# Experts of a decoder layer: weight blocks stationary, rows moving, in the first matrices

## The chip, the cores and the metric
The kernel runs on one core of a Trainium2 chip. The metric is the device time of one execution in microseconds; three executions of the kernel before gave 1971.84, 1976.12 and 1981.54 us, median 1976.12.

## The reference
One decoder layer on x of 8 sequences, 512 tokens, 256 channels: causal self-attention with 16 heads, cross-attention with 16 heads, and then a block with its own small attention, a router and experts. The last of them is what the change touches. After the norm, each of the 4096 tokens goes to two of eight experts:

```
h  = silu(x @ eW1[e].T) * (x @ eW3[e].T)     # 256 -> 256 each
eo = h @ eW2[e].T
out += combine[t, e] * eo                    # for the token's two experts
```

All in float32; the kernel keeps that accuracy with float16 parts: a matrix and its operand are each split into a high and a low part, and a product is three matmuls (high by high, low weight by high operand, high weight by low operand).

## The kernel before
The kernel has three stages, each a block of five engine programs with orders of their own, tied by semaphores: `self_attention`, `cross_attention` with `moe_attention` behind it, and `moe_experts`. The change is in `moe_experts` (lines 2626 to 2920) alone.

Ahead of it, tokens have been written to DRAM sorted by expert, as rows of 256 high parts, 256 low parts and some marks. They are cut into tiles of 128 rows, each of one expert, and two tiles make a pair. There are 40 pairs (NP; 28 of the first six sequences, 12 of the last two), and all loops run over pairs, fully unrolled. Which expert a tile has is known on the chip only: `expert_of` (line 2698) has PE's sequencer load the number from a table in SBUF into a register, and the weights `w13` (first matrices, eW1 and eW3 side by side, 512 columns for each of two 128-row halves kc) and `w2` are addressed with that register. Such a register address is worked out by instructions of PE's sequencer, in the stream between the matmuls.

For a pair p:
- SP loads the two tiles (128 rows each) into `xr` (`first_keys` in the profile, whose memory it uses), up to four pairs ahead.
- PE, `turn_rows` (2692): 8 transposes of 128x128 into `pX`; ACT, `rows_out` (2758), copies them to `xt`.
- PE, `hidden` (2708): for each of the two tiles 6 matmuls, the transposed rows `xt` stationary and 512 columns of `w13` moving, into `pH`: tokens on partitions, 256 values of eW1 and 256 of eW3 along the row. Amid it stand the look-ups of the next pair's experts, and `turn_rows(p + 1)` between the two tiles.
- ACT, `tanh` (2764); DVE, `activate` (2789, 2792), two operations of 512 elements; ACT, `high` (2769); POOL, `low` (2849): the two float16 parts `H16` of the hidden values.
- PE, `turn_hidden` (2725): 8 transposes into `pT`; DVE, `hidden_out` (2798), copies them to `ht`.
- PE, `make` (2736): for each tile 6 matmuls with `ht` stationary and 256 columns of `w2` moving, into `pO`; ACT, `made_out` (2774), to `eo`; POOL, `send_back` (2855), two indirect DMAs a pair to `back` in DRAM.

PE's order is written out by hand: `hidden(p)`, `turn_hidden(p - 1)`, `make(p - 2)`. DVE also works out where results go (`places`, 2817 and 2824), builds a table, and in the last eight or so pairs adds six returned blocks a pair to the residual (`combine`, 2806). Behind the last pair, the rest of the results come back, are combined and stored. A wait is written with `after` (line 28). On PE the waits and the register work run on its sequencer.

Of the kernel before, what the change touches and what calls it, by code (L numbers as in the profile page):

```python
# [8 lines left out]
F16 = mybir.dt.float16  # L9
# [5 lines left out]
P = 128  # L15
T = 512
C = 256
CK = C // P
# [6 lines left out]
def after(eng, sem, n):  # L25

    if n > 0:
        eng.wait_ge(sem, n)

class Names:
# [5 lines left out]
    def sb(self, name, shape, dt):  # L37
        return self.mem.enter_context(self.nc.sbuf_tensor(f"{self.prefix}_{name}", shape, dt))
# [4 lines left out]
    def sem(self, name):  # L43
        return self.keep.enter_context(self.nc.semaphore(f"{self.prefix}_{name}"))
# [2581 lines left out]
def moe_experts(nc, keep, mem, k, x_res, out_dram, B, groups, shared):  # L2626
# [3 lines left out]
    sb, sem = names.sb, names.sem  # L2630

    def banks(name, n):
        return mem.enter_context(nc.psum_tensor(f"e_{name}", [P, n, T], F32))

    w13, w2, weight, back = shared["w13"], shared["w2"], shared["weight"], shared["back"]
# [4 lines left out]
    xt = sb("xt", [P, 2, 2, 2, CK, P], F16)  # L2640
    TH = sb("TH", [P, 2, 2, C], F32)
    H16 = [sb(f"H16_{n}", [P, 2, 2, C], F16) for n in ("hi", "lo")]
    ht = sb("ht", [P, 2, 2, 2, CK, P], F16)
    eo = sb("eo", [P, EB, 2, C], F32)
    odd = sb("odd", [P, IB, 2], F32)
    back_to = sb("back_to", [P, IB, 2], mybir.dt.uint32)
# [2 lines left out]

    pX = banks("pX", 1)  # L2650
    pH = [banks("pH0", 2), banks("pH1", 2)]
    pT = banks("pT", 1)
    pO = [banks("pO0", 1), banks("pO1", 1)]

    s_xt, s_xe, s_h, s_th, s_a, s_hh = sem("xt"), sem("xe"), sem("h"), sem("tanh"), sem("a"), sem("hh")
    s_hi, s_lo, s_ht, s_he, s_o, s_eo = sem("hi"), sem("lo"), sem("ht"), sem("he"), sem("o"), sem("eo")
    s_odd, s_bt = sem("odd"), sem("back_to")
    s_st = [sem(f"stored{n}") for n in range(EB)]
    s_ga, s_cmb, s_out = [sem(f"came_back{n}") for n in range(4)], sem("combined"), sem("out")
# [3 lines left out]
    NP = len(pairs)  # L2663
# [19 lines left out]
    def tensor_program(eng):  # L2683
        expert = {}

        def turn_rows(p):
            eng.wait_ge(s_ld[p % XB], 32 * (p // XB + 1))
            after(eng, s_xe, p)
            for h in range(2):
                for c in range(4):  # L2690
                    o = (h * 4 + c) * P
                    m = eng.transpose(pX[:, 0, :].bitcast(F16)[:, o:o + P], xr[:, p % XB, h, c * P:(c + 1) * P], k.id16[:, :])  # L2692
            m.then_inc(s_xt, 1)

        def expert_of(p, h):
            if p < NP:
                n, q = pairs[p]
                expert[p, h] = eng.value_load(tables.row(n, 0, 2 * q + h), min_val=0, max_val=ER - 1) + 1

        def hidden(p):  # L2700
            eng.wait_ge(s_xe, p + 1)
            after(eng, s_hh, p - 1)
            for h in range(2):
                e = expert[p, h]
                i = 0
                for kc in range(CK):
                    for x, ww in ((0, 0), (0, 1), (1, 0)):
                        m = eng.matmul(pH[p % 2][:, h, :], xt[:, p % 2, h, x, kc, :],  # L2708
                                       w13[ww][:, kc, bass.ds(e, 1), :].rearrange("p a f -> p (a f)"), start=(i == 0), stop=(i == 5))
                        i += 1  # L2710
                        if i == 3:
                            expert_of(p + 1, h)
                if h == 0 and p + 1 < NP:
                    turn_rows(p + 1)
            m.then_inc(s_h, 1)

        def turn_hidden(p):
            eng.wait_ge(s_hi, p + 1)
            eng.wait_ge(s_lo, p + 1)
            after(eng, s_he, p)  # L2720
            for h in range(2):
                for x in range(2):
                    for c in range(CK):
                        o = (h * 4 + x * 2 + c) * P
                        m = eng.transpose(pT[:, 0, :].bitcast(F16)[:, o:o + P], H16[x][:, p % 2, h, c * P:(c + 1) * P], k.id16[:, :])  # L2725
            m.then_inc(s_ht, 1)

        def make(p):
            eng.wait_ge(s_he, p + 1)
            after(eng, s_eo, p - 1)  # L2730
            for h in range(2):
                e = expert[p, h]
                i = 0
                for c in range(CK):
                    for x, ww in ((0, 0), (0, 1), (1, 0)):
                        m = eng.matmul(pO[p % 2][:, 0, h * C:(h + 1) * C], ht[:, p % 2, h, x, c, :],  # L2736
                                       w2[ww][:, bass.ds(e, 1), c, :].rearrange("p a f -> p (a f)"), start=(i == 0), stop=(i == 5))
                        i += 1
            m.then_inc(s_o, 1)

        for h in range(2):
            expert_of(0, h)
        turn_rows(0)
        for p in range(NP):
            hidden(p)
            if p >= 1:
                turn_hidden(p - 1)
            if p >= 2:
                make(p - 2)
        make(NP - 2)  # L2750
        turn_hidden(NP - 1)
        make(NP - 1)

    def scalar_program(eng):
        def rows_out(p):
            eng.wait_ge(s_xt, p + 1)
            after(eng, s_h, p - 1)
            eng.activation(xt[:, p % 2, :, :, :, :].rearrange("p h x k t -> p (h x k t)"), pX[:, 0, :].bitcast(F16),  # L2758
                           ACT.Copy).then_inc(s_xe, 1)

        def tanh(p):
            eng.wait_ge(s_h, p + 1)
            after(eng, s_lo, p - 1)
            eng.activation(TH[:, p % 2, :, :], pH[p % 2][:, :, 0:C], ACT.Tanh, scale=0.5 / WS).then_inc(s_th, 1)

        def high(p):
            eng.wait_ge(s_hh, p + 1)
            after(eng, s_ht, p - 1)
            eng.activation(H16[0][:, p % 2, :, :], TH[:, p % 2, :, :], ACT.Copy).then_inc(s_hi, 1)  # L2769

        def made_out(p):
            eng.wait_ge(s_o, p + 1)
            after(eng, s_st[p % EB], 32 * (p // EB))
            eng.activation(eo[:, p % EB, :, :].rearrange("p h c -> p (h c)"), pO[p % 2][:, 0, :], ACT.Copy).then_inc(s_eo, 1)

        rows_out(0)
        for p in range(NP + 2):
            if p + 1 < NP:
                rows_out(p + 1)
            if p < NP:  # L2780
                tanh(p)
                high(p)
            if p >= 2:
                made_out(p - 2)

    def vector_program(eng):
        def activate(p):
# [3 lines left out]
            eng.wait_ge(s_a, p + 1)  # L2791
            eng.scalar_tensor_tensor(out=TH[:, p % 2, :, :], in0=pH[p % 2][:, :, C:2 * C], scalar=0.5 / WS ** 2,  # L2792
                                     in1=TH[:, p % 2, :, :], op0=ALU.mult, op1=ALU.mult).then_inc(s_hh, 1)

        def hidden_out(p):
            eng.wait_ge(s_ht, p + 1)
            after(eng, s_o, p - 1)
            eng.tensor_copy(ht[:, p % 2, :, :, :, :].rearrange("p h x k t -> p (h x k t)"), pT[:, 0, :].bitcast(F16)).then_inc(s_he, 1)

        def combine(i):  # L2800
            b, t, n = returns[i]
# [28 lines left out]
        for p in range(NP + 2):  # L2830
            if p < NP:
                activate(p)
            if 1 <= p <= NP:
                hidden_out(p - 1)
            if p + 1 < NP:
                places(p + 1)
            for _ in range(TABLED):
                next(table, None)
            if p >= 2:
                for i in returns_at(p - 2):  # L2840
                    combine(i)
# [3 lines left out]
    def gpsimd_program(eng):  # L2845
        def low(p):
            eng.wait_ge(s_hi, p + 1)
            after(eng, s_ht, p - 1)
            eng.tensor_tensor(H16[1][:, p % 2, :, :], TH[:, p % 2, :, :], H16[0][:, p % 2, :, :], ALU.subtract).then_inc(s_lo, 1)  # L2849

        def send_back(p):
            eng.wait_ge(s_eo, p + 1)
            eng.wait_ge(s_bt, 2 * (p + 1))
            for h in range(2):
                eng.indirect_dma_start(out=back[:, :], out_offset=bass.IndirectOffsetOnAxis(ap=back_to[:, p % IB, h:h + 1], axis=0),  # L2855
                                       in_=eo[:, p % EB, h, :], in_offset=None).then_inc(s_st[p % EB], 16)

        def scatter(t):

            b = B - 1  # L2860
            for n in range(2):
                eng.indirect_dma_start(out=groups[1].sent[:, :],
                                       out_offset=bass.IndirectOffsetOnAxis(ap=sent_at[:, b % 2, n, t:t + 1], axis=0),
                                       in_=N2[:, b % 2, t, :],
                                       in_offset=None).then_inc(s_sent[b % 2], 16)

        for p in range(NP + 2):
            if p < NP:
                low(p)
            if p < TT:  # L2870
                scatter(p)
            if p >= 2:
                send_back(p - 2)
# [116 lines left out]
```

## Time and profile before

| | |
|---|---|
| median of three runs | 1976.12 us |
| the profiled execution | 1981.15 us |
| its span, first to last instruction | 1979.4 us |
| PE, DVE, ACT, POOL busy | 90%, 71%, 60%, 55% of the span |
| mean granted clock of TensorE | 0.959 |
| experts: first weight load to last matmul record | 1751.3 to 1960.7 us |

PE is the engine of matmuls and PEld the loads of their stationary operand, which overlap PE. DVE, ACT and POOL are the vector, scalar and GpSimd engines, SP issues DMAs. A q behind an engine's name (PEldq) marks an instruction that only its sequencer handles: register work, waits, table loads. A record of a matmul lasts until its result is out, so records overlap and the pace of PE is read from the starts. Matmuls of one name in a row are merged in the timeline.

### The profile page before, as it was taken

What the parts mean: (1) busy time and instruction counts of PE and PEld (TensorE: products, weight loads), DVE (VectorE), ACT (ScalarE), POOL (GpSimd) and SP (SyncE); (2) the same over time, 40 slices, a digit from 0 to 9 for tenths busy, and PEclk for the clock granted to TensorE, in tenths of its full rate; (3) what the DMA queues carried; (4) which work ended last, traced back from release to release, by engine and by line L of the source; (5) the groups of instructions that cost most, each with busy time, mean ns of one, the idle gap of its engine ahead of it and who ended that gap; (6) DMA issues with size and microseconds to landing.
All of it is one profiled execution on the core that took longest, in us unless ns stands there. A gap on an engine that the chain in (4) does not pass through costs nothing. (4 is left out here: it accounts for less than half of the span.)

```text
span 1979.4 us, 46476 instructions
## 1 busy us (share of the span) xinstructions
PE 1779.3 (90%) x16808; PEld 986.1 (50%) x16808; DVE 1415.2 (71%) x3433; ACT 1185.8 (60%) x2285; POOL 1096.3 (55%) x1102
## 2 busy tenths in 40 slices
PE   5899999999999999889999999986998999779994
PEld 2566767676766767633233333222333344346662
DVE  5766676667676766477777888766699987757677
ACT  2666566566666666367677787782566666435552
POOL 2766666666676666543243433123667776646664
PEclk9999999999999999989899999897999999889998
DMA  6422222223222232321333212301001110224465
GB/s 197 103 66 66 66 66 66 66 66 76 66 66 66 60 82 66 71 65 34 54 65 65 50 37 46 60 11 38 22 23 44 49 49 33 73 73 130 116 209 201
DMA packets 102545, 141.36 MB, mean 71 GB/s; under 512 B 16400, under 2 KB 66352, under 8 KB 102320
## 3 DMA queue, kind: packets, MB, share of 16 engines
q1 hardware_dynamic: 95408, 119.44, 25.6%
q0 software_dynamic: 6912, 18.95, 2.7%
q8 instruction: 138, 2.26, 0.5%
q14 instruction: 87, 0.71, 0.1%
HBM read 53.77 MB, written 33.90 MB: 44 GB/s over the span
## 5 line engine op out<-in xcount | busy, mean ns | idle before, releaser
L821 POOL TENSOR_TENSOR a_P_lo<-a_PR,a_P_hi 128x384 f16<-128x384 f32 (+1 forms) x384 | 378.9, 1001 | 269.7 <-ACT a_PR L630 126.8
L1387 DVE TENSOR_REDUCE x_NM<-x_pm 128x1 f32<-128x512 f32 x512 | 342.5, 688 | 104.0 <-PE x_pm L1123 101.6
L1308 ACT ACTIVATE x_PR<-x_pS 128x512 f32<-128x512 f32 x512 | 300.8, 601 | 118.4 <-PE x_pS L1139 112.5
L739 DVE CUSTOM_DVE_ANT_0 a_pm<-a_pm,a_causal 128x128 f32<-128x128 f32 (+3 forms) x512 | 243.4, 511 | 133.2 <-PE a_pm L511 129.6
L630 ACT ACTIVATE a_PR<-a_pS 128x384 f32<-128x384 f32 (+1 forms) x384 | 202.4, 527 | 148.5 <-PE a_pS L535 145.6
L633 ACT ACTIVATE a_P_hi<-a_pS 128x384 f16<-128x384 f32 (+1 forms) x384 | 203.6, 530 | 26.6 <-PE a_pa L554 26.6
L1151 PE MATMUL x_pa<-x_PR,x_V 128*32 128x256 f32 x2048 | 170.9, 408 | 1.6
L511 PE MATMUL a_pm<-a_KA,a_QA 128*128 128x128 f16 (+3 forms) x512 | 125.3, 305 | 39.4 <-issue 21.6
L533 PE MATMUL a_pS<-a_QA,a_KA 128*128 128x512 f16 (+3 forms) x512 | 153.6, 303 | 1.2 <-ACT a_P_hi L633 0.8
L1462 POOL TENSOR_TENSOR x_res<-x_res,x_OT 128x256 f32<-128x256 f32 x32 | 23.5, 734 | 232.0 <-DVE x_OT L1396 232.0
L534 PE MATMUL a_pS<-a_QB,a_KB 128*128 128x512 f16 (+3 forms) x512 | 148.9, 304 | 0.0
L552 PE MATMUL a_pa<-a_V_hi,a_P_hi 128*128 128x65 f16 x1280 | 135.8, 194 | 0.9 <-POOL a_P_lo L821 0.7
L553 PE MATMUL a_pa<-a_V_lo,a_P_hi 128*128 128x64 f16 x1280 | 135.8, 192 | 0.0
L554 PE MATMUL a_pa<-a_V_hi,a_P_lo 128*128 128x65 f16 x1280 | 134.9, 193 | 0.0
L552 PEld LDWEIGHTS a_pa<-a_V_hi,a_P_hi 128*128 128x128 f16 x1280 | 117.7, 97 | 14.3 <-POOL a_P_lo L821 2.4
L553 PEld LDWEIGHTS a_pa<-a_V_lo,a_P_hi 128*128 128x128 f16 x1280 | 117.1, 98 | 7.2
L554 PEld LDWEIGHTS a_pa<-a_V_hi,a_P_lo 128*128 128x128 f16 x1280 | 117.3, 97 | 0.0
L2708 PE MATMUL e_pH<-m_w_hi,e_xt 128*128 x320 | 109.7, 382 | 1.8 <-ACT e_xt L2758 1.2
L1123 PE MATMUL x_pm<-first_keys,first_queries 48*128 48x512 f16 x256 | 100.8, 410 | 10.1 <-DMA first_queries<-q_k_parts 5.2
L1139 PE MATMUL x_pS<-x_QT,x_KT 49*128 49x512 f16 x256 | 96.9, 397 | 11.3 <-ACT x_PR L1308 10.9
L535 PE MATMUL a_pS<-mask_kq,idb 128*128 128x128 bf16 x512 | 106.6, 221 | 0.0
L1139 PE MATMUL x_pS<-first_queries,first_keys 49*128 49x512 f16 x256 | 97.9, 398 | 8.8 <-ACT x_PR L1308 6.8
(410 smaller groups left out, 5065.6 us busy)
## 6 DMA issues: line engine op xcount, KB each, us to landing
a_QA<-a_nat_q_hi SPq DMA_DIRECT2D x128, 128.0 KB, 2.3
first_keys<-sent SPq DMA_DIRECT2D x80, 129.0 KB
a_KA<-a_nat_k_hi SPq DMA_DIRECT2D x64, 128.0 KB, 2.3
a_KA<-a_nat_k_lo SPq DMA_DIRECT2D x64, 128.0 KB, 2.4
a_QB<-a_nat_q_lo SPq DMA_DIRECT2D x64, 128.0 KB, 2.3
a_KB<-a_nat_k_hi SPq DMA_DIRECT2D x64, 128.0 KB, 2.3
e_ga<-back SPq DMA_DIRECT2D x16, 512.0 KB
first_keys<-in_w SPq DMA_DIRECT2D x12, 512.0 KB
```

What stands on the lines that cost most here:

```text
L533: eng.matmul(o, KA[:, par, side, pair, ks], QA[:, u % RQ, side, pair, qs], start=True, stop=False)
L552: eng.matmul(out, hi, V_hi[:, u % 2, kc, j, 0:D + 1], start=(kc == 0 and t == 0), stop=False, skip_group_check=True)
L553: eng.matmul(out[:, 0:D], hi, V_lo[:, u % 2, kc, j, :], start=False, stop=False, skip_group_check=True)
L554: m = eng.matmul(out, lo, V_hi[:, u % 2, kc, j, 0:D + 1], start=False, stop=(kc == t), skip_group_check=True)
L630: eng.activation(PR[:, m % RF, 0:n], pS[i % 2][:, 0:n], ACT.Exp, scale=SCALE).then_inc(s_e, 1)
L633: eng.activation(P16[0][:, m % RH, 0:n], pS[i % 2][:, 0:n], ACT.Exp, scale=SCALE).then_inc(s_eh, 1)
L739: eng.tensor_tensor_reduce(out=pm[i % 2][:, 0:n], in0=pm[i % 2][:, 0:n], in1=causal[:, T - n:T], scale=1.0, scalar=NEG, op0=ALU.add, op1=A ...
L821: eng.tensor_tensor(P16[1][:, m % RH, 0:n], PR[:, m % RF, 0:n], P16[0][:, m % RH, 0:n], ALU.subtract).then_inc(s_el, 1)
L1139: eng.matmul(pS[i % 2][:, :], KT[par][r, pair, kc * P:(kc + 1) * P], QT[par][r, pair, :], start=True, stop=True).then_inc(s_s, 1)
L1151: m = eng.matmul(pa[2 * D * j:2 * D * (j + 1), q], V[:, b % 2, kc, GH * g + j, :], PR[:, kc, j, q], start=(kc == 0 and half == 0), stop=(k ...
L1308: eng.activation(PR[:, kc, j, :], pS[i % 2][:, :], ACT.Exp, scale=SCALE).then_inc(s_e, 1)
L1387: eng.tensor_reduce(NM[:, v % 2, c:c + 1], ring_bank("max", v, n)[:, :], AX.X, ALU.max, negate=True).then_inc(s_red, 1)
```

## The change
In `hidden`, the operands change places. For each tile and each of four blocks f of 128 columns of `w13` (0 and 1 of eW1, 2 and 3 of eW3), six matmuls run with the 128x128 weight block stationary and the 128 columns of `xt` moving. Results come out with hidden channels on partitions and tokens along the row, at the same places of `pH`, so `tanh`, `activate`, `high` and `low` work on them as before. `H16` is then what `make` needs as its stationary operand. `turn_hidden` and `hidden_out`, the buffers `pT` and `ht` and their semaphores go. `make(p - 2)` stays where it was and waits for `high` and `low`; these now wait for `make(p - 2)` before they overwrite a buffer of `H16`. The look-ups stand between the third and the fourth block.

```diff
--- before.py
+++ after.py
@@ -2640,7 +2640,6 @@
     xt = sb("xt", [P, 2, 2, 2, CK, P], F16)
     TH = sb("TH", [P, 2, 2, C], F32)
     H16 = [sb(f"H16_{n}", [P, 2, 2, C], F16) for n in ("hi", "lo")]
-    ht = sb("ht", [P, 2, 2, 2, CK, P], F16)
     eo = sb("eo", [P, EB, 2, C], F32)
     odd = sb("odd", [P, IB, 2], F32)
     back_to = sb("back_to", [P, IB, 2], mybir.dt.uint32)
@@ -2649,11 +2648,10 @@
 
     pX = banks("pX", 1)
     pH = [banks("pH0", 2), banks("pH1", 2)]
-    pT = banks("pT", 1)
     pO = [banks("pO0", 1), banks("pO1", 1)]
 
     s_xt, s_xe, s_h, s_th, s_a, s_hh = sem("xt"), sem("xe"), sem("h"), sem("tanh"), sem("a"), sem("hh")
-    s_hi, s_lo, s_ht, s_he, s_o, s_eo = sem("hi"), sem("lo"), sem("ht"), sem("he"), sem("o"), sem("eo")
+    s_hi, s_lo, s_o, s_eo = sem("hi"), sem("lo"), sem("o"), sem("eo")
     s_odd, s_bt = sem("odd"), sem("back_to")
     s_st = [sem(f"stored{n}") for n in range(EB)]
     s_ga, s_cmb, s_out = [sem(f"came_back{n}") for n in range(4)], sem("combined"), sem("out")
@@ -2702,38 +2700,30 @@
             after(eng, s_hh, p - 1)
             for h in range(2):
                 e = expert[p, h]
-                i = 0
-                for kc in range(CK):
-                    for x, ww in ((0, 0), (0, 1), (1, 0)):
-                        m = eng.matmul(pH[p % 2][:, h, :], xt[:, p % 2, h, x, kc, :],
-                                       w13[ww][:, kc, bass.ds(e, 1), :].rearrange("p a f -> p (a f)"), start=(i == 0), stop=(i == 5))
-                        i += 1
-                        if i == 3:
-                            expert_of(p + 1, h)
+                for f in range(2 * CK):
+                    i = 0
+                    for kc in range(CK):
+                        for x, ww in ((0, 0), (0, 1), (1, 0)):
+                            m = eng.matmul(pH[p % 2][:, h, f * P:(f + 1) * P],
+                                           w13[ww][:, kc, bass.ds(e, 1), f * P:(f + 1) * P].rearrange("p a f -> p (a f)"),
+                                           xt[:, p % 2, h, x, kc, :], start=(i == 0), stop=(i == 5))
+                            i += 1
+                    if f == CK:
+                        expert_of(p + 1, h)
                 if h == 0 and p + 1 < NP:
                     turn_rows(p + 1)
             m.then_inc(s_h, 1)
 
-        def turn_hidden(p):
+        def make(p):
             eng.wait_ge(s_hi, p + 1)
             eng.wait_ge(s_lo, p + 1)
-            after(eng, s_he, p)
-            for h in range(2):
-                for x in range(2):
-                    for c in range(CK):
-                        o = (h * 4 + x * 2 + c) * P
-                        m = eng.transpose(pT[:, 0, :].bitcast(F16)[:, o:o + P], H16[x][:, p % 2, h, c * P:(c + 1) * P], k.id16[:, :])
-            m.then_inc(s_ht, 1)
-
-        def make(p):
-            eng.wait_ge(s_he, p + 1)
             after(eng, s_eo, p - 1)
             for h in range(2):
                 e = expert[p, h]
                 i = 0
                 for c in range(CK):
                     for x, ww in ((0, 0), (0, 1), (1, 0)):
-                        m = eng.matmul(pO[p % 2][:, 0, h * C:(h + 1) * C], ht[:, p % 2, h, x, c, :],
+                        m = eng.matmul(pO[p % 2][:, 0, h * C:(h + 1) * C], H16[x][:, p % 2, h, c * P:(c + 1) * P],
                                        w2[ww][:, bass.ds(e, 1), c, :].rearrange("p a f -> p (a f)"), start=(i == 0), stop=(i == 5))
                         i += 1
             m.then_inc(s_o, 1)
@@ -2743,12 +2733,9 @@
         turn_rows(0)
         for p in range(NP):
             hidden(p)
-            if p >= 1:
-                turn_hidden(p - 1)
             if p >= 2:
                 make(p - 2)
         make(NP - 2)
-        turn_hidden(NP - 1)
         make(NP - 1)
 
     def scalar_program(eng):
@@ -2765,7 +2752,7 @@
 
         def high(p):
             eng.wait_ge(s_hh, p + 1)
-            after(eng, s_ht, p - 1)
+            after(eng, s_o, p - 1)
             eng.activation(H16[0][:, p % 2, :, :], TH[:, p % 2, :, :], ACT.Copy).then_inc(s_hi, 1)
 
         def made_out(p):
@@ -2791,11 +2778,6 @@
             eng.wait_ge(s_a, p + 1)
             eng.scalar_tensor_tensor(out=TH[:, p % 2, :, :], in0=pH[p % 2][:, :, C:2 * C], scalar=0.5 / WS ** 2,
                                      in1=TH[:, p % 2, :, :], op0=ALU.mult, op1=ALU.mult).then_inc(s_hh, 1)
-
-        def hidden_out(p):
-            eng.wait_ge(s_ht, p + 1)
-            after(eng, s_o, p - 1)
-            eng.tensor_copy(ht[:, p % 2, :, :, :, :].rearrange("p h x k t -> p (h x k t)"), pT[:, 0, :].bitcast(F16)).then_inc(s_he, 1)
 
         def combine(i):
             b, t, n = returns[i]
@@ -2830,8 +2812,6 @@
         for p in range(NP + 2):
             if p < NP:
                 activate(p)
-            if 1 <= p <= NP:
-                hidden_out(p - 1)
             if p + 1 < NP:
                 places(p + 1)
             for _ in range(TABLED):
@@ -2845,7 +2825,7 @@
     def gpsimd_program(eng):
         def low(p):
             eng.wait_ge(s_hi, p + 1)
-            after(eng, s_ht, p - 1)
+            after(eng, s_o, p - 1)
             eng.tensor_tensor(H16[1][:, p % 2, :, :], TH[:, p % 2, :, :], H16[0][:, p % 2, :, :], ALU.subtract).then_inc(s_lo, 1)
 
         def send_back(p):
```

## Rows read from the trace of the kernel before

**Rows 1.** Groups by line, 1751 to 1965: busy us, mean ns | idle before.
```profile
L2764 ACT ACTIVATE e_TH<-e_pH 128x512 f32<-128x512 f32 x40 | 23.9, 597 | 7.9 <-PE e_pH L2708 7.6 <-issue 0.3
```

**Rows 2.** Busy us (instructions) of PE, PEld, DVE, ACT, POOL, then PEclk, DMA.
```profile
1840.00:1860.00 20.00, 20.00 (x167) 13.41 (x166) 13.42 (x30) 11.53 (x17) 13.06 (x14) 1.00 0.39 111
...
1950.00:1965.00 15.00, 5.38 (x52) 4.22 (x52) 9.01 (x18) 2.84 (x6) 10.55 (x10) 1.00 0.35 118
```

**Rows 3.** Timeline of PE, one round: start us, us.
```profile
1850.25 0.28 PE L2725 MATMUL e_pT<-id,e_H_hi 128*128 128x128 f16 x2
...
1850.70 0.27 PE L2736 MATMUL e_pO<-m_w_hi,e_ht 128*128 x1
...
1852.01 0.38 PE L2708 MATMUL e_pH<-m_w_hi,e_xt 128*128 x1
...
1853.30 0.61 PE L2692 MATMUL e_pX<-id,first_keys 128*128 128x128 f16 x8
...
1855.05 0.28 PE L2725 MATMUL e_pT<-id,e_H_hi 128*128 128x128 f16 x2
```

**Rows 4.** Lines 2708 and 2736, whole trace: ns min/median/max, first and last start.
```profile
L2708 PEld LDWEIGHTS e_pH<-m_w_hi,e_xt x320: 95/98/152, 1753.5 to 1949.1; 128*128 128x128 f16 x160
...
L2708 PEldq FUSED_REGOPS  x160: 46/56/65, 1753.4 to 1947.3; - x160
L2708 PEldq ALU_OP  x160: 32/32/42, 1753.6 to 1947.4; - x160
...
L2736 PEldq ALU_OP  x240: 32/32/32, 1766.0 to 1959.9; - x120
...
L2736 PEldq FUSED_REGOPS  x80: 46/46/46, 1766.2 to 1959.8; - x80
```

**Rows 5.** The sequencer in one `make` and in one `hidden` without look-ups.
```profile
L2736 PEldq ALU_OP  x6: 32/32/32, 1854.6 to 1855.4; - x6
L2736 PEldq FUSED_REGOPS  x2: 46/46/46, 1854.8 to 1855.3; - x2
...
L2708 PEldq FUSED_REGOPS  x4: 46/53/60, 1946.5 to 1947.3; - x4
L2708 PEldq ALU_OP  x4: 32/32/32, 1946.7 to 1947.4; - x4
```

**Rows 6.** Lines 2698, 2708 and 28, one round (1850.85 to 1855.64).
```profile
L2698 PEldq TENSOR_LOAD <-m_table x2: 418/488/559, 1851.2 to 1852.8; - x2
...
L2708 PEldq FUSED_REGOPS  x4: 46/53/60, 1850.9 to 1853.6; - x4
...
L28 PEldq EVENT_SEMAPHORE  x5: 51/51/633, 1850.8 to 1855.6; - x5
```

**Rows 7.** Timeline of PE, 1935 to 1962.
```profile
1936.70 0.39 PE L2708 MATMUL e_pH<-m_w_hi,e_xt 128*128 x1 [0.29 <-issue]
...
1949.34 0.38 PE L2708 MATMUL e_pH<-m_w_hi,e_xt 128*128 x1
```

**Rows 8.** Timeline of PE in the first attention, 300 to 303.
```profile
300.16 0.19 PE L552 MATMUL a_pa<-a_V_hi,a_P_hi 128*128 128x65 f16 x1
...
300.44 0.33 PE L511 MATMUL a_pm<-a_KA,a_QA 128*128 128x128 f16 x2
```

**Rows 9.** Timeline of DVE, one round of the last seven.
```profile
1936.13 0.68 DVE L2789 SCALAR_TENSOR_TENSOR e_TH<-e_TH,e_pH 128x512 f32<-128x512 f32 x1
...
1937.45 0.68 DVE L2798 COPY e_ht<-e_pT 128x1024 f16<-128x1024 f16 x1
...
1941.82 0.68 DVE L2789 SCALAR_TENSOR_TENSOR e_TH<-e_TH,e_pH 128x512 f32<-128x512 f32 x1
```

**Rows 10.** Line 2698, 1935 to 1943.
```profile
L2698 PEldq TENSOR_LOAD <-m_table x4: 302/630/1064, 1935.5 to 1942.3; - x4
```

**Rows 11.** Timeline of POOL, the end of the stage.
```profile
1955.32 1.26 POOL L2849 TENSOR_TENSOR e_H_lo<-e_TH,e_H_hi 128x512 f16<-128x512 f32 x1 [1.64 <-ACT e_H_hi L2769]
...
1963.38 0.96 POOL L2855 DMA_INDIRECT back<-e_eo,e_back_to  x1 [0.30 <-issue]
```

## The prediction
> **What bounds the kernel now.** I read the page first, for span and busy shares; the diff touches only the last stage, the experts. Then the groups by line of that stage: the lines of PE lead it, and what ACT, DVE and POOL do for a pair is short, as the tanh of 597 ns, 40 times [rows 1]. Then the view by windows. In a middle stretch (1840 to 1860) PE is busy 20.00 of 20 us at a granted clock of 1.00, which is the 2.4 GHz level; DVE, ACT and POOL are at 13.4, 11.5 and 13.1 us [rows 2]. So a round, one pair of tiles, is set by PE. The timeline of PE shows what a round is made of, if one reads starts and not durations (records of matmuls overlap): the eight transposes of the hidden values start at 1850.25, the twelve matmuls of the second matrices at 1850.70, the next `hidden` at 1852.01, and the next transposes of hidden values at 1855.05 [rows 3]. So 0.45 us for 8 transposes (56 ns each), 1.31 us for 12 matmuls of 256 columns, and 3.04 us for a `hidden` with the 8 transposes of rows inside it, 0.45 of it for them, 2.59 for its 12 matmuls of 512 columns (0.216 each). The round is 4.80 us.
>
> The array is not all of PE, though. Instructions reach it through PE's sequencer, whose rows (PEldq) the views by source line show. The expert's number is a register, so every distinct address of a weight block takes one register instruction: 160 FUSED_REGOPS and 160 ALU_OP for `hidden`, that is 8 a pair, and 80 and 240 for `make`, again 8 a pair [rows 4]. A pair has 12 + 12 matmuls in these two; each third one re-uses the address of the block's high part. They last 32 to 60 ns, but what counts is from start to start. In a `make` where the sequencer was not held, the eight start between 1854.6 and 1855.4; in a `hidden` without look-ups, between 1946.5 and 1947.4 [rows 5]. That is 0.8/7 and 0.9/7 us, 0.11 to 0.13 us; I take 0.12. The matmuls between them add nothing that can be seen: there is one matmul behind every first address and two behind every second.
>
> The two look-ups of the next pair's experts (L2698) are dearer: a TENSOR_LOAD of 418 or 559 ns, then register work and an assert; from 1852.8 to the next address at 1853.6 is 0.8 us around a load of 0.42, the last of the two, so the load plus some 0.37 [rows 6]. Five waits on semaphores lie in the round's window, 51 ns each unless they are really held [rows 6]; with the pause behind them I put 0.12 each. Per pair now: 16 x 0.12 = 1.92, two look-ups 2 x (0.49 + 0.37) = 1.72, four or so waits 0.48: 4.1 us of 4.80. The sequencer has 0.7 us to spare per pair, and where one look-up was slow the array already stood still: the matmul at 1936.70 has 0.29 us idle before it, released by "issue" [rows 7].
>
> **The change, part by part.**
>
> *`hidden`, array.* The 12 matmuls of 512 columns become 48 of 128, the same columns in all. At the transposes' 56 ns [rows 3] that is 2.69 us instead of 2.59: plus 0.10. Every one now has its own weight load. Bounds for a matmul of 128 columns with fresh weights: below, the first attention's strings of nine with 64 or 65 columns and a fresh 128x128 block each, which start at 300.16 and are over at 300.44, 31 ns apiece [rows 8], so that the load itself can keep up with 56 ns; above, the full record of a weight load one after another, 98 ns [rows 4], 4.70 us a pair. I take 56, since the transposes are the same shapes. In a sentence apart: the Trainium skill, "TensorE: Matmul & The Clock Gate", section Back-to-back issue gap, states about 81 ns for a sustained stream of loads and matmuls at 128 columns; by it `hidden` would take 3.89 us of array, 1.3 more than now; the strings at 31 ns in this trace speak against it.
>
> *`hidden`, sequencer.* The weight block's address now depends on f as well. Four f, two kc, two parts, two tiles: 32 distinct addresses a pair instead of 8. The order (0,0), (0,1), (1,0) re-uses the high part only within one f and kc, so nothing more is saved. Plus 24 x 0.12 = 2.88 us. The cover of 0.7 us does not hold that.
>
> *Transposes of hidden values.* PE loses 8 transposes and 0.45 us of array, the sequencer one wait (0.12). DVE loses `hidden_out`, a copy of 0.68 us [rows 9].
>
> *`make`.* The same 12 matmuls, the same addresses. It reads H16 directly and waits for high and low parts, which are a round old: 4 us after the end of their `hidden`, and two rounds are between. Nothing on the path.
>
> *New waits on s_o in `high` and `low`.* They want `make(p - 2)`, which PE issues straight behind `hidden(p)` and ends 1.3 to 1.5 us after it. `high(p)` is only possible 0.2 + 0.6 + 1.4 = 2.2 us after `hidden(p)` (start-up, tanh [rows 1], two DVE operations of 0.68 to 0.7 [rows 9]), so the wait is over by then; were it late, ACT's `made_out` and `rows_out` would be queued behind it, and PE's next `hidden` behind those. Cost 0, at most some tenths of a us in a round at half clock.
>
> *Freed `pT` and `ht`.* Nobody else takes them: 0.
>
> **The sum.** Array per round: 2.69 + 0.45 + 1.31 = 4.45 us. Sequencer: 32 x 0.12 = 3.84; look-ups 2 x (0.35 + 0.37) = 1.44; two waits 0.24: 5.52 for `hidden`; `make` 8 x 0.12 + 0.16 (one wait or two) = 1.12. Together 6.64 us. For the load I take 0.35, between the shortest, 302, and the 418 to 559 of a full round, since with the queue to the array empty nothing should hold it up [rows 6, 10]. So the sequencer becomes the bound, at 6.64 against 4.80.
>
> Up to the end of the last `hidden`: 40 `hidden` and, since `make` runs two pairs behind, 37 `make`. 40 x 5.52 + 37 x 1.12 - 1.6 (the last one looks nothing up and turns no rows) = 260.6 us. The first address of the stage is at 1753.4 [rows 4], hence 2014.0. Now the last matmul of `hidden` starts at 1949.34 and ends at about 1949.7 [rows 7]: plus 64.3 us. This already holds that DVE sets the last seven rounds now, at 5.69 us (1936.13 to 1941.82) [rows 9]: without the copy it needs 5.0, less than the sequencer.
>
> The end gets shorter. The last low part starts at 1955.32 and ends at 1956.6, 6.9 us after the last `hidden`, since six combines stand ahead of the activation on DVE [rows 9, 11]; with slack on DVE it is 0.2 + 0.6 + 1.4 + 0.7 + 1.25 = 4.2 us. The six sends behind it (last one at 1963.38) [rows 11] are as before. Minus 2.7.
>
> Plus 61.6 us. The profiled execution took 1981.15 us for its span of 1979.4, 5.0 us over the median of 1976.12; it becomes 2042.8, and against the median 1976.12 + 61.6 = 2037.7, say 2038.
>
> Ends of the terms: an address at 0.112 and loads of 0.30 give 6.3 us a round (2024); loads of 0.63, the median of a stretch with much DMA traffic (up to 1.06) [rows 10], in every round give 7.2 (2060).
>
> **The rivals.**
>
> A. *The sequencer stays ahead and only the array counts* (faster). Then a round is 4.45 instead of 4.80 (33 x 0.35 = 11.5), the last seven save DVE's copy (7 x 0.68 = 4.8), the end 2.7: minus 19, 1957 us. It decides if the sequencer's 4.1 - 0.12 us with the new addresses stay below 4.45, that is 24 addresses under 20 ns each. For it: PE's busy share. Against it: start to start they take 110 ns or more everywhere [rows 5]. 8%.
>
> B. *Weight loads set the pace.* 98 ns each: 4.70 + 0.45 + 1.31 = 6.46 a round, 33 x 1.66 + 7 x 0.77 - 2.7 = 57 us, 2034 us, hard to tell by the time alone, but the idle time would lie between loads. The Trainium skill's 81 ns (same page and section) gives an array of 5.65 and, alone, 33 x 0.85 - 2.7 = 25 us, about 2002. Against both: rows 8. It also takes the sequencer being ahead. 5%.
>
> C. *The clock falls.* The array's columns would fill 4.45 of 6.64 us, 67%. At the 1.2 GHz level a round is about 2 x 4.3 = 8.6 us and the time 1976 + 33 x 3.8 + 7 x 2.9 - 3 = some 2120. Against it: from 1950 to 1965 PE is busy 5.38 of 15 us and the clock is 1.00 [rows 2]. 6%.
>
> D. *The address work is smaller than I count* (one instruction for several blocks) and it comes out level: some 14 to 17 register instructions for a pair in `hidden` where I count 32. 3%.
>
> **How the numbers follow.** The forecast has 78%, with its own range of 2022 to 2060. 2020 to 2062 holds it but for a few, and B's upper form. What a measurement can tell from no change is about 0.5%, 10 us: faster 0.09 (A, part of D), same 0.03, slower 0.88.
>
> **What would show it.** Right: the stage's rounds at 6.4 to 6.9 us; FUSED_REGOPS and ALU_OP of the line of `hidden` 1280 in all; matmuls in threes with a gap, idle time of PE before them put down to "issue", some 2 us a round; DVE, ACT and POOL all with more idle time; clock 1.00. Wrong: register instructions below 1000, rounds under 5 us, or gaps before every single matmul (B), or records of 250 ns and more at 128 columns (C).

## The result
The changed kernel took 2038.43 us (median of 4, 2030.15 to 2051.55) against 1975.85 before, a ratio of 1.0321 (95% interval 1.0259 to 1.0382): 63 us slower, where 62 were forecast.

### The profile page after: what moved, and what is told of

The parts are those of the page before. It is cut to its first block and busy times, and to the rows that moved or that the text cites. A ratio compares the mean times of both kernels' runs of the same rounds, so it can differ in the third digit from the quotient of the medians.

```text
span 2034.3 us, 49560 instructions
## 1 busy us (share of the span) xinstructions
PE 1803.8 (89%) x17928; PEld 1047.7 (52%) x17928; DVE 1366.8 (67%) x3393; ACT 1186.6 (58%) x2285; POOL 1096.5 (54%) x1102
## 5 line engine op out<-in xcount | busy, mean ns | idle before, releaser
L2707 PE MATMUL e_pH<-e_xt,m_w_hi 128*128 128x128 f16 x1280 | 162.2, 222 | 43.4 <-issue 42.1
L2707 PEld LDWEIGHTS e_pH<-e_xt,m_w_hi 128*128 x1280 | 115.7, 97 | 64.0 <-issue 56.8
L2776 DVE SCALAR_TENSOR_TENSOR e_TH<-e_TH,e_pH 128x512 f32<-128x512 f32 x40 | 27.5, 688 | 163.1 <-ACT e_TH L2751 124.4
L2707 PE MATMUL e_pH<-e_xt,m_w_lo 128*128 128x128 f16 x640 | 130.6, 218 | 0.2
L2829 POOL TENSOR_TENSOR e_H_lo<-e_TH,e_H_hi 128x512 f16<-128x512 f32 x40 | 46.7, 1168 | 132.0 <-ACT e_H_hi L2756 132.0
```

The lines of the kernel that those rows point to most:

```text
L2707: m = eng.matmul(pH[p % 2][:, h, f * P:(f + 1) * P], w13[ww][:, kc, bass.ds(e, 1), f * P:(f + 1) * P].rearrange("p a f -> p (a f)"), xt[:, ...
```

## The profile after
First two lines of the page (busy us, share of the span, instructions), then the view by windows, with the columns of [rows 2].

```profile
span 2034.3 us, 49560 instructions
...
PE 1803.8 (89%) x17928; PEld 1047.7 (52%) x17928; DVE 1366.8 (67%) x3393; ACT 1186.6 (58%) x2285; POOL 1096.5 (54%) x1102
```

```profile
1840.00:1860.00 20.00, 16.96 (x208) 14.40 (x206) 5.60 (x18) 8.23 (x13) 9.19 (x9) 1.00 0.33 101
```

In the same stretch as in [rows 2] PE is busy 16.96 us instead of 20.00, at an unchanged clock of 1.00 (2.4 GHz), DVE 5.6 instead of 13.4, ACT 8.2 instead of 11.5, POOL 9.2 instead of 13.1: no engine is full any more. The count of instructions on PE went up by 1120 on the page, to 17928. What PE waits for is in the view of waits (in total us, times, longest) of the stage:

```profile
PE e_pH L2707 <- issue: 41.7, 77, 1.4
...
PE e_pO L2726 <- POOL e_H_lo L2829: 1.7, 1, 1.7
```

```profile
1880.36 0.22 PE L2707 MATMUL e_pH<-e_xt,m_w_lo 128*128 128x128 f16 x1
1880.41 0.30 PE L2707 MATMUL e_pH<-e_xt,m_w_hi 128*128 128x128 f16 x2
1880.60 0.22 PE L2707 MATMUL e_pH<-e_xt,m_w_lo 128*128 128x128 f16 x1
1880.65 0.22 PE L2707 MATMUL e_pH<-e_xt,m_w_hi 128*128 128x128 f16 x1
1881.36 0.23 PE L2707 MATMUL e_pH<-e_xt,m_w_hi 128*128 128x128 f16 x1 [0.49 <-issue]
1881.47 0.22 PE L2707 MATMUL e_pH<-e_xt,m_w_lo 128*128 128x128 f16 x1
1881.53 0.29 PE L2707 MATMUL e_pH<-e_xt,m_w_hi 128*128 128x128 f16 x2
...
1881.97 0.27 PE L2726 MATMUL e_pO<-m_w_hi,e_H_hi 128*128 x1
...
1888.52 0.27 PE L2726 MATMUL e_pO<-m_w_hi,e_H_hi 128*128 x1
```

The two starts of `make` are 6.55 us apart; the round before was 4.80 [rows 3]. In between, matmuls come in threes, as the third re-uses an address: low part at 1880.36, low part again at 1880.60, 0.24 us for three matmuls of 128 columns which the array could do in 0.17. At the look-up the next matmul starts 0.71 us after the one before it (1880.65 to 1881.36), and PE is idle for 0.49 of it. The sequencer's rows by source line, whole trace (ns min/median/max, first and last start), to be compared with [rows 4], [rows 6] and [rows 10]:

```profile
L2707 PEldq FUSED_REGOPS  x640: 46/46/65, 1743.6 to 2007.7; - x160
L2707 PEldq ALU_OP  x640: 32/32/42, 1743.7 to 2007.9; - x160
...
L2726 PEldq ALU_OP  x320: 32/32/32, 1760.3 to 2013.5; - x160
...
L2696 PEldq TENSOR_LOAD <-m_table x80: 296/301/1147, 1739.9 to 2001.6; - x80
```

640 and 640 address instructions in `hidden` instead of 160 and 160, as counted ahead; the look-ups' loads fell from a median of 424 ns to 301. The pace of the addresses, in a piece of `hidden` without look-up or wait (1886 to 1887.19):

```profile
L2707 PEldq FUSED_REGOPS  x5: 46/46/46, 1886.0 to 1887.0; - x5
L2707 PEldq ALU_OP  x5: 32/32/32, 1886.1 to 1887.1; - x5
```

Ten of them start between 1886.0 and 1887.1, 0.12 us apart. The end of the stage, from the timelines of PE and POOL, to be compared with [rows 7] and [rows 11]:

```profile
2008.00 0.22 PE L2707 MATMUL e_pH<-e_xt,m_w_hi 128*128 128x128 f16 x1
...
2011.05 1.45 POOL L2829 TENSOR_TENSOR e_H_lo<-e_TH,e_H_hi 128x512 f16<-128x512 f32 x1 [1.29 <-ACT e_H_hi L2756]
...
2018.99 0.96 POOL L2835 DMA_INDIRECT back<-e_eo,e_back_to  x1 [0.30 <-issue]
```

The last `hidden` ends at 2008.2, its low part is done at 2012.5, 4.3 us later (6.9 before), and the last send starts 10.8 us after that `hidden` (13.7 before).

**How long the stage takes.** The stages ahead of the experts are the same code, but their length differs from one execution to the next: the first look-up of PE started at 1749.8 in the profiled execution before, and at 1739.9 in the one after.

```profile
L2698 PEldq TENSOR_LOAD <-m_table x80: 295/424/1064, 1749.8 to 1942.3; - x80
```

So I read every kernel by the stretch from its first look-up to the end of the span, one profiled execution each: 229.6 us before, 294.4 after, plus 64.8 (and minus 9.9 ahead of the stage, in code that the change leaves as it was, which is why the spans differ by 54.9 only). The ratios of the timed runs, against executions of the kernel before made alongside, stand beside it.

## The experiments
The theory: PE's sequencer sets the round, since every distinct address of a weight block behind a register costs it 0.12 us, with the look-ups and waits in the same stream. Its rivals: the weight loads set the pace; register operands or the swapped roles are slow as such; the array stays the bound (A). "Stage" is the stretch just described, "round" the median distance from one `make` to the next in the timeline of PE. e1 to e4 use wrong expert weights for some or all tiles (e2 the wrong blocks of them), so they show where the time goes and are no versions to use.

| kernel | ratio to before (95%) | stage, us | round, us |
|---|---|---|---|
| before | 1 | 229.6 | 4.79 |
| the change | 1.0321 (1.0259 to 1.0382) | 294.4 | 6.66 |
| e1, constant experts | 0.9916 (0.9884 to 0.9949) | 210.7 | 4.44 |
| e2, one block four times | 0.9928 (0.9889 to 0.9967) | 212.0 | 4.44 |
| e3, first look-ups alone | 0.9916 (0.9886 to 0.9945) | 210.5 | 4.44 |
| e4, before, constant experts | 1.0007 (0.9971 to 1.0043) | 228.7 | 4.79 |
| e5, before, matmuls cut in four | 1.0407 (1.0367 to 1.0446) | 299.3 | 6.82 |
| e6, one tile of two swapped | 1.0104 (1.0052 to 1.0157) | 244.1 | 5.31 |
| e7, before, late copies on ACT | 0.9975 (0.9945 to 1.0006) | 226.1 | 4.79, late 5.1 |
| e8, the change, look-ups twice | 1.0601 (1.0539 to 1.0662) | 349.7 | 8.04 |
| e9, before, look-ups twice | 1.0104 (1.0070 to 1.0139) | 249.1 | 5.39 |
| e10, e7 with the end reordered | 1.0010 (0.9983 to 1.0036) | 224.4 | 4.79, late 5.1 |

**e1: no addresses at all.**
```diff
-                expert[p, h] = eng.value_load(tables.row(n, 0, 2 * q + h), ...) + 1
+                eng.value_load(tables.row(n, 0, 2 * q + h), ...)
+                expert[p, h] = 1 + (2 * p + h) % ER
```

> The changed kernel, with each tile's expert a constant of the program instead of a register (some tiles thus use another expert's weights); the look-ups still run, their values are not used. The same 48 + 12 matmuls and loads a pair, no address instruction at all. If address instructions set the round: the sequencer needs some 2 us, the array's 4.45 us bind, 1957 us (1950 to 1964), 80 us under the change. If weight loads set it: 98 ns each leave it at about 2034, 81 ns each at about 2002.

It came out 0.84% under before and the stage 83.7 us under the change's. One round in the timeline of PE, from the first matmul of a `make` to the next, and the longest wait of PE:

```profile
1846.96 0.27 PE L2727 MATMUL e_pO<-m_w_hi,e_H_hi 128*128 128x256 f16 x1
...
1851.40 0.27 PE L2727 MATMUL e_pO<-m_w_hi,e_H_hi 128*128 128x256 f16 x1
```

```profile
PE e_pO L2727 <- POOL e_H_lo L2830: 4.8, 2, 3.9
```

4.44 us a round, with the 48 loads and matmuls of the change all there; the array's own 4.45 of the prediction. Of the 41.7 us of idle time on "issue" 0.3 is left. Both weight-load theories (2002 and 2034) are out.

**e2: the same matmuls and registers, 8 addresses a pair instead of 32.**
```diff
-  ... w13[ww][:, kc, bass.ds(e, 1), f * P:(f + 1) * P] ...
+  ... w13[ww][:, kc, bass.ds(e, 1), 0:P] ...
```

> The changed kernel, with all four blocks f of a product taken from the first block of the weights (so the hidden values of the other three are wrong). Same matmuls, loads, look-ups and a register in every address, but 4 distinct addresses per tile in `hidden`, as before the change: 8 a pair instead of 32. If the count of address instructions sets the round: sequencer 4.0 us, under the array's 4.45, 1957 us (1950 to 1966). If a stationary operand behind a register is slow to load, or loads set the pace: 2034 to 2038, no change.

```profile
1848.06 0.27 PE L2726 MATMUL e_pO<-m_w_hi,e_H_hi 128*128 x1
...
1852.50 0.27 PE L2726 MATMUL e_pO<-m_w_hi,e_H_hi 128*128 x1
```

```profile
L2707 PEldq FUSED_REGOPS  x160: 46/56/65, 1746.2 to 1923.4; - x160
```

160 instead of 640 (and 160 ALU_OPs likewise), and the round is 4.44 us again. Matmuls, loads, look-ups and register operands are those of the change; only the number of distinct addresses is another. This is the sharpest of the runs: a register operand costs nothing that the round shows, working out an address does.

**e3: registers worked out once.**
```diff
-                expert[p, h] = eng.value_load(...) + 1
+                expert[p, h] = eng.value_load(...) + 1 if p == 0 else expert[0, h]
```

> The changed kernel, with the look-ups of the first pair alone; all pairs use the first pair's two experts. The addresses stay in registers, but each is worked out once in the whole stage and kept. Sequencer theory: nothing left but waits, array-bound, 1957 us (1948 to 1964), the same as with fixed addresses. Weight-load theories: 2002 or 2034. If register operands themselves were slow on the way to the array: near 2038.

```profile
L2707 PEldq FUSED_REGOPS  x16: 46/46/65, 1738.6 to 1742.5; - x16
```

Rounds of 4.44 us (16 + 16 address instructions in `hidden` in the whole trace, 2 loads), 210.5 us for the stage. As e1, from the other side: look-ups and addresses are gone, but all operands are still behind registers.

**e4: before without addresses, the control.** The edit is that of e1.

> The kernel before, with the expert of each tile a constant of the program and the look-ups kept (some tiles use another expert's weights). Control: before the change the array binds and the sequencer has slack, so taking its 16 address instructions a pair away gives nothing: 1974 us, within 0.4% of before. If the sequencer already bound part of the round, 10 us or more under before.

1.0007 (0.9971 to 1.0043), rounds of 4.79 us. Before the change the sequencer's 16 addresses a pair cost nothing that can be measured.

**e5: the roles as before, the addresses of the change.**
```diff
+                for f in range(2 * CK):
...
+                            m = eng.matmul(pH[p % 2][:, h, f * P:(f + 1) * P], xt[:, p % 2, h, x, kc, :],
+                                           w13[ww][:, kc, bass.ds(e, 1), f * P:(f + 1) * P]...)
```

> The kernel before, with its operands as they were (rows stationary, weights moving), transposes and copy included, but each matmul of 512 columns cut into four of 128 in the order of the change: 32 addresses a pair. Sequencer theory: the round is the change's 6.66 us and one more wait, 6.8 us; the end of the stage as long as before: 2038 + 5 + 3 = 2046 us (2036 to 2054). If swapping the operands is what costs, the array's 4.9 us bind: 1980 us (1976 to 1986).

```profile
1842.98 0.27 PE L2738 MATMUL e_pO<-m_w_hi,e_ht 128*128 x1
...
1849.76 0.27 PE L2738 MATMUL e_pO<-m_w_hi,e_ht 128*128 x1
```

```profile
L2709 PEldq FUSED_REGOPS  x640: 46/46/65, 1743.7 to 2011.5; - x160
```

```profile
PE e_pH L2709 <- issue: 40.0, 76, 0.9
```

6.78 us for this round against 6.8 expected, and 69.7 us more for the stage against 70. The timed ratio of 1.0407 (1.0367 to 1.0446) is above the 1.035 of the forecast and just above the upper end of its range, 1.0395; the stage does not show what the other 10 us are. The swap is not what costs; the cut into blocks that each need an address is. With e2 this shows it both ways.

**e6: half the change.**
```diff
+                if h == 0:     # swapped, 4 blocks of 128
...
+                else:          # as before, 512 columns
```

> Half the change: of each pair the first tile with the operands swapped, the second as before with its 4 transposes and half the copy. 16 + 4 addresses in `hidden` and 8 in `make`. Sequencer theory: 20 x 0.118 + 0.9 + look-ups 1.3 + waits 0.6 + 0.2 = 5.3 us a round against 4.62 of array: 1976 + 33 x 0.5 - 7 x 0.35 - 1 = 1989 us (1982 to 1998). If the cost grew with the number of swapped matmuls alone: half of 62, 2007 us. If it has a threshold elsewhere: 1966 to 1972, half of rival A's gain.

```profile
1843.24 0.27 PE L2748 MATMUL e_pO<-m_w_hi,e_H_hi 128*128 x1
...
1848.55 0.27 PE L2748 MATMUL e_pO<-m_w_hi,e_H_hi 128*128 x1
...
1853.73 0.27 PE L2748 MATMUL e_pO<-m_w_hi,e_H_hi 128*128 x1
```

```profile
L2710 PEldq FUSED_REGOPS  x320: 46/46/65, 1742.8 to 1952.9; - x160
```

Rounds of 5.31 and 5.18 us, with 320 + 320 addresses for the swapped tiles; 14.5 us more for the stage against the expected 13. A cost in proportion to the swapped matmuls would be 32 us, and a round of some 5.7. The timed ratio, 1.0104 with an interval up to 1.0157 (31 us), does not rule that out by itself; the rounds and the stage do. What the first part of the added work costs is hidden in the sequencer's slack.

**e8 and e9: look-ups twice.** One more line in `expert_of`, `eng.value_load(...)` again with its value unused, in the change and in the kernel before.

> The changed kernel, with every look-up done a second time, its value unused: 80 more TENSOR_LOADs with their bounds check and assert, nothing more for the array. Where the sequencer sets the round, each of them is paid in full: 0.30 + 0.06 + 0.21 + 0.08 = 0.64 us, 1.28 a round: 2038 + 51 = 2089 us (2080 to 2100), round 7.9 us. If only the pace of the address work mattered to the array and the look-ups were hidden behind queued matmuls: 2038.

```profile
1842.24 0.27 PE L2727 MATMUL e_pO<-m_w_hi,e_H_hi 128*128 x1
...
1850.35 0.27 PE L2727 MATMUL e_pO<-m_w_hi,e_H_hi 128*128 x1
```

8.04 us a round (8.11 here), 1.38 more than in the change, 55.3 us for the stage against 51: paid in full and 8% more. (The four terms expected for a look-up, 0.30, 0.06, 0.21 and 0.08, add up to 0.65 and not to 0.64, 1.30 a round.) In the change, work added to the sequencer is on the path from its first instruction.

> The kernel before with the same second look-ups. It measures the slack that the prediction put at 0.7 us a round: the sequencer's 4.1 us, or 3.7 with loads of 0.30, become 5.0 to 5.4, against 4.79 of array. Sequencer theory: a round of 5.0 to 5.3 us, and little in the last seven rounds, where DVE has 5.68: 33 x 0.2 to 33 x 0.5, 7 to 17 us over before (ratio 1.003 to 1.009). If the slack were over 1.3 us: no change.

```profile
1846.33 0.27 PE L2737 MATMUL e_pO<-m_w_hi,e_ht 128*128 x1
...
1851.73 0.27 PE L2737 MATMUL e_pO<-m_w_hi,e_ht 128*128 x1
...
1857.22 0.27 PE L2737 MATMUL e_pO<-m_w_hi,e_ht 128*128 x1
```

5.40 and 5.49 us here, 5.39 in the median. Of the same 1.28 us the kernel before pays 0.6, so that it had 0.7 us of slack: the figure of the prediction. The round is over the 5.0 to 5.3 expected, and so is the total: 19.5 us of stage against 7 to 17, a timed ratio of 1.0104 against 1.003 to 1.009.

**e7 and e10: without the addresses.** What the change gives on DVE can be had alone, with the copy of transposed values on ACT in the last nine pairs:
```diff
-            if 1 <= p <= NP:
+            if 1 <= p <= NP and p - 1 < LATE:      # DVE; LATE = NP - 9
...
+            if LATE <= p - 1 < NP:                  # ACT, behind high(p)
+                hidden_out(p - 1)
```

> Not a test of the cause, but a version that keeps what the change could bring without its addresses: the kernel before, with the copy of the transposed hidden values moved from DVE to ACT in the last nine pairs, where DVE sets the round at 5.69 us. DVE then needs 5.0 us, the array 4.8: 7 x 0.68 = 4.8 us less and something at the end, 1969 to 1973 us. If ACT's order delays the copy (it stands behind the high part): no gain or up to 3 us more.

The late rounds fell from 5.68 to 5.12 us by DVE's starts, not to 5.0, and the stage by 3.5 us. The timeline of DVE shows where the rest went:

```profile
1923.29 0.23 DVE L2832 SCALAR_TENSOR_TENSOR e_back_to<-first_keys,e_odd 128x1 uint32<-128x1 f16 x2
1923.44 3.35 DVE L2814 SCALAR_TENSOR_TENSOR x_res<-e_ga,m_weight,x_res 128x256 f32<-128x256 f32 x6
```

Six combines take 3.35 us, where they took 2.45 before; the two small `back_to` operations take 0.23 where they took 1.09. The 0.9 us are the same, they have only gone to a neighbour. Against before the interval (0.9945 to 1.0006) reaches 1.

e10 also puts the combines of pair 38 behind the activation of pair 39 (DVE) and the output of pair 38 ahead of the last copy (ACT).

> The version with the copy on ACT in the last nine pairs, and two orders changed at the very end: on DVE the six combines of pair 38 go behind the activation of pair 39, and on ACT the output of pair 38 is copied out before the last copy of transposed values. Rounds as in the version without it (5.12 us at DVE's pace); from the last `hidden` to the last send some 12 us instead of 14.8 there and 13.7 before. Together 5 to 7 us under before, ratio 0.9965 to 0.9975; if POOL's six sends take over the whole end, 0.998.

From the last `hidden` to the last send it takes 11.9 us, as expected, where e7 took 14.2 (not the 14.8 of the text above). Its stage is the shortest of the kernels that compute the layer, 224.4 us, 5.2 under before, but the timed ratio is 1.0010 (0.9983 to 1.0036), above the 0.9965 to 0.9975 expected. A gain of 5 us in one stage is less than what the stages ahead of it vary: their length was 1749.8 us in the profiled execution before and 1739.9 in the one after. So no version that beats the kernel before has been shown.

## Why the prediction was right
- *The sequencer as the bound.* Right in mechanism: e2, e5, e8 and e9 show it from four sides. The forecast round was 6.64 us, the measured one 6.66, but that they are so close is partly luck, as the next points show.
- *An address at 0.12 us, 32 a pair.* Right, in count (1280) and in pace, but for pauses that come on top.
- *Look-ups.* The load was taken at 0.35 us and the work around it at 0.37; they are 0.30 and 0.35. `make` came slightly cheaper too: all its eight addresses are ALU_OPs now (320, no FUSED_REGOPS). With 40 addresses at 0.12 (4.8), two look-ups at 0.64 and three waits at 0.12 this makes 6.44 us, not 6.64.
- *What fills it up to 6.66* was not in the sum: pauses of the sequencer, which I did not foresee. In the rows of the line of `hidden` from 1889.9 to 1890.3, a FUSED_REGOPS starts at 1889.9 and the next address, with no wait and no look-up between, at 1890.2:

```profile
L2707 PEldq FUSED_REGOPS  x1: 46/46/46, 1889.9 to 1889.9; - x1
L2707 PEldq ALU_OP  x1: 32/32/32, 1890.2 to 1890.2; - x1
```

This one is 0.15 us over the usual distance. Added up from start to start over 29 rounds of the trace (1780 to 1980), a round is 4.06 us for the 32 addresses of `hidden` (forecast 3.84), 0.94 for the 8 of `make` (0.96), 1.31 for two look-ups (1.44) and 0.35 for three waits (0.40), together 6.66. Distances behind an address that are over 40 ns longer than the usual one come 2 to 3 times a round and make 0.24 us. They fit e8, where the added work cost 1.38 us and not 1.30. The two errors, look-ups too dear and pauses left out, cancel; that is luck. The pauses' cause was not tried.
- *Two long rounds* were not in the sum either. From the first address to the end of the last `hidden` it had 260.6 us; the trace has 264.6 (1743.6 to 2008.2). Of the 4.0 us between, 2.8 are two rounds of 8.29 and 7.79 us. In the first, the sequencer's rows have 1.5 us between two addresses (1778.9 to 1780.5), with no wait and no look-up between, and PE goes idle:

```profile
1780.46 0.22 PE L2707 MATMUL e_pH<-e_xt,m_w_hi 128*128 128x128 f16 x1 [1.20 <-issue]
```

The second has the longest look-up load, 1147 ns, at 1984.3. The cause of both is open.
- *The array at 4.45 us, beneath it.* Right: 4.44 in e1 to e3. A matmul of 128 columns with a fresh block goes at 56 ns (median from start to start in `hidden`, e1 to e3), not at a full load record of 98. The Trainium skill, "TensorE: Matmul & The Clock Gate", section Back-to-back issue gap, gives about 81 ns for a sustained stream of loads and matmuls of 128 columns; the 56 ns of these traces do not agree with it. Rival A's price, minus 19 us, is what e1 and e3 gained in their stage (18.9 and 19.1), but not where A had it: there the end is no shorter than before (14.0 us from the last `hidden` to the last send, against 13.7), and the 18.6 and 18.8 us are all gained up to the last `hidden`. A failed by its condition; that its total fits is in part luck.
- *The end*, minus 2.7 us: measured 10.8 instead of 13.7 from the last `hidden` to the last send, minus 2.9.
- *The new waits, `make`, the freed buffers* at nothing: no wait of PE on them in the change but one of 1.7 us at the last pair, whose low part `make` has to wait for in any order.
- *The last seven rounds.* Right that DVE no longer sets them in the change. But its floor of 5.0 us was too low by 0.1, as e7 shows (5.12); it did not count here.
- *The ends of the range.* By its own terms (40 addresses 0.008 us cheaper, two loads 0.05 cheaper) the lower end is a round of 6.22 us and not 6.3, some 2021 us and not 2024; nothing hangs on it.
- *The signs to look for* came as named but one: idle time of PE on "issue" is 41.7 us, 1.1 a round and not some 2, since gaps between threes are shorter than the tail of a matmul's record and count as busy; only those at look-ups show.
- *The clock* stayed at 1.00, the 2.4 GHz level, in the middle stretches (1840 to 1860), with PE's columns filling 4.45 of 6.66 us: rival C did not come.

## What to carry to other kernels
Where an engine is full in the profile, read its sequencer's rows as well: start to start, not their durations, and count what one round issues. In this kernel a block addressed through a register costs an instruction of 0.12 us for every distinct address, so cutting a matmul into smaller ones can cost more than the work it saves, even if the array does not mind. Adding a known amount of unused sequencer work to the kernel (e9) measures the slack before a change spends it.

## What was not expected of the hardware
- The look-up's load took a median of 424 ns where PE was busy without a gap (before) and 301 to 302 where it was not (after, e5, e6). e1, e2 and e4 have an array as full and yet 304, 306 and 302, so that alone is not the reason; what is, was left open.
- Small DVE operations lasted several times as long beside POOL's `low`. In the timeline of before, two of one element each:

```profile
1853.24 1.15 POOL L2849 TENSOR_TENSOR e_H_lo<-e_TH,e_H_hi 128x512 f16<-128x512 f32 x1 [1.24 <-ACT e_H_hi L2769]
...
1853.39 1.09 DVE L2824 SCALAR_TENSOR_TENSOR e_back_to<-first_keys,e_odd 128x1 uint32<-128x1 f16 x2
```

They end at 1854.48, 0.09 us after `low`. The groups by line of the stage (busy us, mean ns), of before and of after:

```profile
L2824 DVE SCALAR_TENSOR_TENSOR e_back_to<-first_keys,e_odd 128x1 uint32<-128x1 f16 x78 | 41.8, 574 | 1.3
```

```profile
L2806 DVE SCALAR_TENSOR_TENSOR e_back_to<-first_keys,e_odd 128x1 uint32<-128x1 f16 x78 | 8.9, 155 | 1.4
```

574 ns in the mean against 155 for the same operation. In e7 the combines pay instead. That the two engines hold each other up is read from these times; it was not tried by itself.
